# Local attention's projections and its rounds put into one block

## The reference, cut to what matters

```python
g = x @ Wg.T + bg
v = x @ Wv.T + bv
# per head:
dot = jnp.einsum('bhid,bhjd->bhij', g, g)
corr = dot / (nrm[..., :, None] * nrm[..., None, :] + 1e-08)
corr = (corr * m + 1.0) / 2.0                 # m: j <= i and j >= i - 128
gene_means = jnp.mean(corr, axis=3)
denom = gene_means + 0.5
sum_inv = jnp.sum(1.0 / denom, axis=2, keepdims=True)
gene_fitness = 1.0 / (denom * sum_inv)
weighted = corr * gene_fitness[..., None]
attn = softmax(weighted * m + (1.0 - m) * NEG)
out = attn @ v
```

## Time and profile before

| what | value |
|---|---|
| median of three runs | 2852.92 us (2851.32 to 2854.34) |
| the profiled execution | 2852.49 us |
| its span | 2850.7 us |
| PE busy | 2644.2 us (93%) |
| DVE busy | 1940.7 us (68%) |
| ACT, POOL busy | 802.1, 799.2 us (28%, 28%) |
| mean granted clock of PE | 0.97 |

### The profile page before, as it was taken

How to read it: one execution, slowest core, us unless ns; L and a number is a source line. 1 busy time by engine, 2 the same in 40 slices (tenths; PEclk the granted TensorE clock), 3 DMA queues, 4 the chain that set the end, 5 groups by cost and what they waited for, 6 DMA issues and landing times. The chain is left out here.

```text
span 2850.7 us, 39066 instructions
## 1 busy us (share of the span) xinstructions
PE 2644.2 (93%) x14094; PEld 1608.4 (56%) x14094; DVE 1940.7 (68%) x3503; ACT 802.1 (28%) x1239; POOL 799.2 (28%) x795
## 2 busy tenths in 40 slices
PE   7999988999998999679888859999999999999996
PEld 3444544555554455335445526777777777777774
DVE  4788404666666344268888737888888888888884
ACT  1111312333332233267777601111111111111110
POOL 1222104544553333356666411111111111111000
PEclk9999999999999999889999979999999999999998
DMA  5344130000000233323233430111111111111111
GB/s 161 132 161 154 60 109 1 1 1 1 1 1 0 79 101 102 91 91 91 84 88 90 144 76 25 44 45 43 43 43 43 44 44 45 44 45 44 41 37 33
DMA packets 220884, 177.07 MB, mean 62 GB/s; under 512 B 40171, under 2 KB 185579, under 8 KB 219670
## 3 DMA queue, kind: packets, MB, share of 16 engines
q1 hardware_dynamic: 183710, 147.87, 17.3%
q10 hardware_dynamic: 36984, 26.71, 3.5%
HBM read 90.51 MB, written 52.43 MB: 50 GB/s over the span
## 5 line engine op out<-in xcount | busy, mean ns | idle before, releaser
L1974 PE MATMUL bank<-tiles,tl_XQT 128*128 128x512 f32 (+1 forms) x768 | 331.7, 575 | 7.5 <-DMA tl_XQT<-tl_QB 4.8
L1989 PE MATMUL bank<-tiles,tl_HT 128*128 128x512 f32 x704 | 317.8, 607 | 20.2 <-DMA tl_HT<-tl_tmp 20.2
L1979 PE MATMUL bank<-tiles,tl_XQT 128*128 128x512 f32 (+1 forms) x768 | 317.9, 557 | 0.0
L1989 PEld LDWEIGHTS bank<-tiles,tl_HT 128*128 128x128 f32 x704 | 225.2, 324 | 97.2 <-issue 30.2
L1974 PEld LDWEIGHTS bank<-tiles,tl_XQT 128*128 128x128 f32 x768 | 232.5, 310 | 73.9 <-issue 16.3
L1979 PEld LDWEIGHTS bank<-tiles,tl_XQT 128*128 128x128 f32 x768 | 236.7, 308 | 65.6
L1477 POOL TENSOR_SCALAR_AFFINE_SELECT tiles<-tiles 128x512 f32<-128x512 f32 x256 | 173.0, 678 | 194.5 <-ACT tiles L1650 138.3
L1927 POOL TENSOR_TENSOR tl_rs<-tl_ve,mhalf 128x1 f32<-128x1 f32 x32 | 17.7, 552 | 593.0 <-DVE tl_ve L2082 593.0
L2023 ACT ACTIVATE tl_HQ<-bank 128x512 f32<-128x512 f32 (+1 forms) x96 | 54.0, 562 | 427.5 <-PE bank L1974 405.7
L1710 DVE SCALAR_TENSOR_TENSOR tiles<-tiles,bank 128x1024 f32<-128x1024 f32 (+1 forms) x128 | 141.6, 1147 | 4.9 <-PE bank L1559 2.7
L1919 POOL TENSOR_TENSOR tl_rs<-tl_ve,mhalf 128x1 f32<-128x1 f32 x32 | 19.9, 623 | 426.6 <-DVE tl_ve L2064 426.6
(11 more groups left out here) (287 smaller groups left out, 5069.8 us busy)
## 6 DMA issues: line engine op xcount, KB each, us to landing
tl_HT<-tl_tmp SPq DMA_DIRECT2D x256, 44.0 KB, 1.9
tl_HT<-tl_tmp ACTq DMA_DIRECT2D x256, 44.0 KB, 1.9
fp_weights<-space_quant ACTq DMA_DIRECT2D x33, 256.0 KB, 2.2
X<-in_x SPq DMA_DIRECT2D x8, 1024.0 KB, 11.9
v<-la_VS SPq DMA_DIRECT2D x32, 256.0 KB, 2.3
unit_g<-la_GH SPq DMA_DIRECT2D x32, 256.0 KB, 2.9
unit_gT<-la_GT SPq DMA_DIRECT2D x32, 256.0 KB, 3.2
la_GN<-unit_g SPq DMA_DIRECT2D x128, 64.0 KB, 2.2
```

Of the source, the lines that this page charges most:

```text
L1974: mm = e.matmul(bank[(2 * q) % 3][:, 0:w], chunk(XQT[n % 2], c), WgT[q][:, :, c, :], start=(c == 0), stop=(c == C - 1))
L1979: mm = e.matmul(bank[(2 * q + 1) % 3][:, 0:w], chunk(XQT[n % 2], c), WuT[q][:, :, c, :], start=(c == 0), stop=(c == C - 1))
L1989: mm = e.matmul(bank[DOWN][:, :], chunk(HT, q), WdT[:, q, :], start=(q == 0), stop=(q == IC - 1))
```

## The change

- `local_attention_projections` goes away as a stage. Its work is in `local_attention`, half a tile per round: `projected(p)` gives the tile m = p // 4 + 10 and the part. Part 0 has the transposition of x of tile m + 1 and the matmuls with Wg of tile m; part 1 the transposition of the unit vectors of tile m - 1 and the matmuls with Wv of tile m. The log norms are kept for a batch element (8 tiles) and split, transposed and stored once per batch element.
- The rounds now start at s = -56: 22 rounds (p = -44 to -2) have projections alone, then each round has half a tile, until p = 90.
- The projections' PSUM banks are 0 to 3, one each for x, g, v and the unit vectors, which are those of the dot products. PE's `projections` waits until DVE has taken this round's dot products; `dots` waits until ACT and DVE have emptied the projections' banks. `projections` stands between `arguments(p + 1)` and `attend(x + 1)`.
- AHEAD is 12 (was 16), RING 16 (was 20); the gather runs two steps behind the arguments (was four), and z, sums, inverse and scaled come earlier in a chunk: sums at p = 6 and 10 of a chunk (were 8 and 12), the first scaling at 10 (was 14), the second at 12 (was 16).
- ACT does `exp(s + 1)` ahead of `tanh(p + 1)`, and the normaliser last. POOL has the same order of masks and the power behind them.
- The constants are made during the first rounds, before p = 0.
- The output weights and the down weights are loaded at p = 98, the latter into the eleven buffers of the projections; gate and up weights at s = 118, 122 and 124.
- The local weights get a home (`k.home`) that outlives `Spaces`, and Wo and the folded weights go there afterwards.

The core of the diff:

```diff
+RING = 16
+BUFFERS = 11
+GATE_AT = [4 * q * SLOT for q in range(3)]
+UP_AT = [4 * q * SLOT + C * w for q, (_, w) in enumerate(PIECES)]
+DOWN_AT = RING * SLOT
...
+LAST_IN = (3, 7, 10)
...
+    AHEAD, LAG, BEFORE = 12, 2, 10
...
+        XT = [piece(n).rearrange("p (c t) -> p c t", c=C) for n in range(2)]
+        Gs, SG, GH, VS, GQ = ([piece(n + i) for i in range(m)] for n, m in ((2, 2), (4, 1), (5, 2), (7, 2), (9, 2)))
...
+        ROUNDS = range(-AHEAD - 4 * BEFORE - 4, NS + LAG + 2, 2)
+        projected = lambda p: (p // 4 + BEFORE, p // 2 % 2)
+        batch_next = lambda p: (p + 2) // (G * C) if (p + 2) % (G * C) == 0 and 0 <= p + 2 < NS else None
+        batch_of = lambda m: m // G - 1 if m % G == 0 and 0 < m <= NT else None
...
+                def projections_stored(m, part):
+                    if part == 0:
+                        if tile(m - 1):
+                            n = m - 1
+                            e.wait_ge(s_vc.sem, s_vc.at(n + 1))
+                            e.dma_start(by_tile(k.VNd, n), VS[n % 2].rearrange("p (c d) -> p c d", c=C)).then_inc(d_v[n % 2].sem, 16)
+                        if tile(m - 2):
+                            n = m - 2
+                            e.wait_ge(s_gc.sem, s_gc.at(n + 1))
+                            e.dma_start(k.GTd[:, n // G * C:(n // G + 1) * C, n % G * P:(n % G + 1) * P],
+                                        GQ[n % 2].rearrange("p (c t) -> p c t", c=C)).then_inc(d_gq[n % 2].sem, 16)
+                        b = batch_of(m - 1)
+                        if b is not None:
+                            for h in range(2):
+                                e.wait_ge(s_yc.sem, s_yc.at(2 * b + h + 1))
+                                e.dma_start(k.YD[b][:, half_of(h)], YT[h][:, :]).then_inc(d_y[h].sem, 16)
+                    elif tile(m - 1):
+                        n = m - 1
+                        e.wait_ge(s_gh.sem, s_gh.at(n + 1))
+                        e.dma_start(by_tile(k.GNd, n), GH[n % 2].rearrange("p (c d) -> p c d", c=C)).then_inc(d_gh[n % 2].sem, 16)
...
+                def weights_after_projections():
+                    for s in (s_v, s_gh, s_s2, s_gt):
+                        e.wait_ge(s.sem, s.at(NT))
+                    VB, WoT = k.out_weights
+                    e.dma_start(VB, k.SW[:, VO_AT:FOLDED]).then_inc(s_next.sem, 16)
+                    e.dma_start(WoT[:, :, :], chunked(a["L1_attn_Wo_T"])).then_inc(s_next.sem, 16)
+                    for j in range(4):
+                        e.dma_start(k.tiles[32 * j:32 * j + 32, DOWN_AT:DOWN_AT + IC * D].rearrange("p (i d) -> p i d", d=D),
+                                    down_rows[32 * IC * j:32 * IC * (j + 1), :].rearrange("(i p) d -> p i d", p=32)).then_inc(k.d_wd, 16)
...
+                    b = batch_next(p)
+                    if b is not None:
+                        batch_stored(b)
+                        if b:
+                            e.wait_ge(s_arg.sem, s_arg.at(G * (C * b - 1)))
+                        load_rows(C * b)
+                    projections_stored(*projected(p))
...
+                        m, part = projected(x + AHEAD)
+                        e.wait_ge(s_xc.sem, s_xc.at(min(m + 1 + part, NT)))
+                        e.wait_ge(s_ga.sem, s_ga.at(min(m + part, NT)))
+                        e.wait_ge(s_vc.sem, s_vc.at(min(m, NT)))
+                        e.wait_ge(s_gc.sem, s_gc.at(min(m - 1, NT)))
+                        e.wait_ge(s_yc.sem, s_yc.at(2 * min((m - 1) // G, B)))
...
+                def projections(m, part, s):
+                    e.wait_ge(s_u.sem, s_u.at(min(s + 2, NS)))
+                    if part == 0:
+                        if tile(m + 1):
+                            n = m + 1
+                            e.wait_ge(s_xc.sem, s_xc.at(n))
+                            e.wait_ge(s_yc.sem, s_yc.at(2 * ((m - 1) // G)))
+                            for c in range(C):
+                                mm = e.transpose(bank[0][:, c * P:(c + 1) * P], tile_x(n)[:, c * P:(c + 1) * P], k.ident[:, :])
+                            mm.then_inc(s_t.sem, 1)
+                        if tile(m):
+                            e.wait_ge(s_xc.sem, s_xc.at(m + 1))
+                            e.wait_ge(s_ga.sem, s_ga.at(m))
+                            for c in range(C):
+                                mm = e.matmul(bank[1][:, :], XT[m % 2][:, c, :], WgT[:, c, :], start=(c == 0), stop=(c == C - 1))
+                            mm.then_inc(s_g.sem, 1)
+                    else:
+                        if tile(m - 1):
+                            n = m - 1
+                            e.wait_ge(s_gh.sem, s_gh.at(n + 1))
+                            e.wait_ge(s_gc.sem, s_gc.at(n))
+                            for c in range(C):
+                                mm = e.transpose(bank[3][:, c * P:(c + 1) * P], GH[n % 2][:, c * P:(c + 1) * P], k.ident[:, :])
+                            mm.then_inc(s_gt.sem, 1)
+                        if tile(m):
+                            e.wait_ge(s_vc.sem, s_vc.at(m))
+                            for c in range(C):
+                                mm = e.matmul(bank[2][:, :], XT[m % 2][:, c, :], WvT[:, c, :], start=(c == 0), stop=(c == C - 1))
+                            mm.then_inc(s_v.sem, 1)
+                        b = batch_of(m)
+                        if b is not None:
+                            e.wait_ge(s_y.sem, s_y.at(b + 1))
+                            e.wait_ge(s_xc.sem, s_xc.at(min(m + 2, NT)))
+                            e.wait_ge(s_ga.sem, s_ga.at(min(m + 1, NT)))
+                            for h in range(2):
+                                for q in range(HG):
+                                    g = HG * h + q
+                                    mm = e.transpose(bank[h][0:3 * H, q * P:(q + 1) * P],
+                                                     Y3[:, g * H:(g + 1) * H, :].rearrange("p h s -> p (h s)"), k.ident[:, :])
+                                mm.then_inc(s_yt.sem, 1)
...
-                    chains = [(at_chunk(p, G + HG * h), h) for h in range(2)]
+                    chains = [(at_chunk(p, 6 + HG * h), h) for h in range(2)]
...
-                    if there(p - 4):
-                        gather(p - 4)
-                        gather(p - 3)
+                    if there(p - 2):
+                        gather(p - 2)
+                        gather(p - 1)
...
+                    projections(*projected(p), s)
...
                         exp(s)
+                        exp(s + 1)
                     if there(p):
                         tanh(p + 1)
+                    if part == 0:
+                        if tile(m + 1):
+                            x_transposed(m + 1)
+                        if b is not None:
+                            logarithms(b)
+                    else:
+                        if tile(m - 1):
+                            unit_transposed(m - 1)
+                        if tile(m):
+                            v_scaled(m)
+                        if b is not None:
+                            y_transposed(b)
                     if there(x) and not first(x):
                         normaliser(x // 2)
-                    if there(s):
-                        exp(s + 1)
...
+                    if p == 0:
+                        constants()
                     if there(x):
                         out(x // 2)
                     if there(s):
                         scores(s)
                         scores(s + 1)
-                    if here(G + 6) is not None:
-                        scaled(here(G + 6), 0)
-                    if here(2 * G) is not None:
-                        scaled(here(2 * G), 1)
-                    if here(HG + 2) is not None:
-                        z(here(HG + 2), 0)
-                    if here(G + 2) is not None:
-                        z(here(G + 2), 1)
-                        inverse(here(G + 2), 0)
-                    if here(G + 4) is not None:
-                        inverse(here(G + 4), 1)
-                        share(here(G + 4))
+                    if part == 1 and tile(m):
+                        norms(m)
+                    if here(12) is not None:
+                        scaled(here(12), 1)
                     if here(HG) is not None:
-                        tile_sums(here(HG), 0)
+                        z(here(HG), 0)
+                        tile_sums(here(HG), 1)
+                    if here(6) is not None:
+                        inverse(here(6), 0)
                     if here(G) is not None:
-                        tile_sums(here(G), 1)
+                        z(here(G), 1)
+                    if here(0) is not None:
+                        tile_sums(here(0), 0)
+                    if here(10) is not None:
+                        inverse(here(10), 1)
+                        share(here(10))
+                        scaled(here(10), 0)
+                    if part == 0:
```

(7 more changed lines are left out.)

370 lines of the change are left out of this document (144 added, 226 removed).

## The result

| | before | after |
|---|---|---|
| median of the plain runs | 2852.12 us (2850.71 to 2854.34) | 2824.14 us (2822.50 to 2826.00) |
| ratio, 95% interval | | 0.9901 (0.9884 to 0.9919) |
| span of the profiled execution | 2850.7 us | 2822.0 us |
| start of the block to the first dot products | 315.5 us | 129.0 us |
| the 38 rounds s = 0 to 74 | 236.6 us | 386.9 us |

A forecast was written before the change was run, and what follows sets the result against it. PE was taken to bound the projections, while steady attention left it holes (busy 88.42 of 100 us). From 2852.5 us, -192.4 + 151.2 - 2 + 4 - 10.9 = -50.1 gave 2802 us, range 2774 to 2834.

The forecast's parts named there:

- the half-price lock: POOL's power blocks DVE at half its full price, slack absorbing the rest: 2830 us; chance 0.18 shared with non-sharing rounds.
- rounds that don't share at all: Double rounds keep all old holes plus new waits, 10.9 us each: 2829 us; chance 0.18 shared with the half-price lock.
- (a, b): Prologue and run-up together: 123.1 us to the first dot products against 315.5 before, 192.4 us less.
- (c): 38 rounds s = 0 to 74 with attention and half tiles: 10.2 us each against 6.22, 151.2 us more.
- (d): Rounds s = 76 to 130 without projections: 2 us gained; bulk weight load at p = 98: 4 us lost (0 to 8).
- (e): End of the block: last store no longer queues behind the down weights, 10.9 us saved.
- (a): Prologue, p = -44 to -2: ten projection tiles, 82.1 us, plus 2 us for the first batch's rows; constants covered.
- (b): Run-up of the attention ring: six rounds instead of eight, 6.5 us each with about 0.5 of waits, 39 us.
- The sharing itself gives next to nothing: Rounds with both cost what the stages cost apart (6.22 + 3.9 = 10.1), new hand-overs eating the closed holes.
- PE at full (9.6): PE stays full in double rounds because copies hide behind `attend`; the tail keeps 5 us more: 2774 us; chance 0.14.
- The lock: POOL's 2.9 us power blocks DVE; full price 55 us over 19 tiles, 2857 us, chance 0.02.
- Rival 3: Banks 0 to 3: PE waits for both late DVE scores and the copy; 12.2 us per round, 2878 us; chance 0.06.

The follow-up runs named there:

- first experiment: The changed kernel with the six output and down weight transfers issued one per round from p = 98 to 108, not all at p = 98: 2805.57 us.
- the last experiment: The early Tanh kernel (2801.4 us) with a batch's log-norm transpositions on TensorE and copies on ScalarE moved ahead of V: 2801.73 us.
- third experiment: The changed kernel with BEFORE = 34 instead of 10, so all 32 projection tiles run ahead of the first attention round: 2830.53 us.
- early Tanh: The kernel with first and last weights spread one transfer per round (2802.5 us), plus an unread one-column Tanh right behind the logarithm: 2801.36 us.
- the experiment: The changed kernel with POOL doing a second, unread power of the same shape after each inverse norm: 2822.48 us.

## Why the prediction was right and wrong

The forecast was 2802 and the measurement is 2824.14: inside the stated range, outside the 2783 to 2821 that I gave the forecast itself. The range went up to 2834 for the half-price lock and for rounds that don't share at all (both about 2830, with a chance of 0.18), and neither came true: the rounds with both took the 10.2 us that I had. So the right range is luck. Where the 22 us went is in the table, against what the traces show, in us of span (the start of the block, 1.1 later, and the stages behind, 1.9 longer, make up the 28.7, to rounding):

| term | said | measured |
|---|---|---|
| (a, b) to the first dot products | -192.4 | -186.5 |
| (c) 38 rounds with both | +151.2 | +150.3 |
| (d) tail without the bulk load | -2 | -4.4 (first experiment) |
| (d) bulk load | +4 (0 to 8) | +16.5 |
| (e) end | -10.9 | -7.7 |

**(a) held.** The first arguments run at 1011.65, 83.5 us after the block's start; I had 84.1 with the 2 us for the rows' round trip. The round trip costs nothing, though barely: the last experiment turned it into 1.02 us. The parts are a little other than mine. A plain tile takes 7.75 us, and the tile with the log norms of a batch 1.9 more, which my 4 us for the start covered. The constants cost nothing either; without the cover of further tiles 10.6 us come back (third experiment).

**(b) failed by 6.5 us.** PE's busy part was near what I had, 37.36 us against 36. The waits were 8.1 us against my 3. I had taken "about 0.5 of waits" from nothing but the thought that a half tile fills them. But the half tile stands behind `arguments(p + 1)`, which waits for the tanh of p: 6.6 of the 8.1 us by PE's waits, 2.5 of them at p = 0, with a table load in it. Three of the 6.5 us are that table load (the versions without it and with the early Tanh); the rest did not go away with another order on PE.

**(c) held**, by its steps as well: busy 9.59 per round for my 9.48 + 0.1, waits 0.6 for my 0.2 + 0.4. The copy's cover by `attend(x + 1)` is 0.5 us (I had 0.58), and without it a round is 10.71. "The sharing itself gives next to nothing" is right for these rounds: it costs 3.3 us in 387. A batch costs 2.4 us, not 1.5. The table loads are 1.4 of the 2.4 (the version without them), so with two of them in my 1.5 I had priced them too low.

**The rivals.** PE at full (9.6) was rightly set against: the dot products wait 0.5 us per round. The lock, with a chance of 0.02 in full and a share of 0.18 in half, did not show. The trace of the change bears out the reason that I had given: beside the 19 powers in these rounds DVE has no operation with two SBUF inputs. Whether larger ones would be held up is not shown; the ten small ones of the experiment were not. Rival 3 was right in place, price (12.2; 12.16 measured) and effect (slower than before), but needs another order than the one written. That the price agrees so well is luck, since its cause is only in part what I gave: PE's waits for DVE's late scores are 25.1 us of it, while those before the dot products, for ACT's copy behind a late tanh among others, grew by some 41. Its total, 2914.65, is above my 2878 because of 37.5 us in the tail, where the call waits for the scores with nothing to do.

**(d) failed on the size of the bulk load**, and this is the main error: 12.5 of the 21 us of span that were missing. The step was "some 14 us stand before the next GN loads", against a lead of 8 to 10 us. From the first issue (1484.05) to the landing of the load that PE wanted (1507.08) it is 23.0 us, 9 more than my 14. And PE wanted it 7.7 us after that first issue, 2 earlier than my 10. Of these 7.7 us the load itself had only 3.3, for SP needs 4.4 us to issue the weights in front of it.

The 14 us were nowhere in the rows that I had. They mean some 340 GB/s for all of it, but the down pieces go to 32 partitions each, and the row "0.91 of DMA time at 172 GB/s" was of just these. SP's wait of 13.0 us was of these four pieces alone in front of one store, and 1.8 MB more now stand ahead of them. The throughput of the kernel after is 365 to 394 GB/s while Wo lands, then about 190 to 230 for the down pieces: 2.8 MB at 200 GB/s are 14 us, with 1.8 MB at some 370 GB/s it is 19, and the loads behind landed when that was over. The Trainium skill, "SBUF — State Buffer", section "Can I just issue two DMAs to hit both halves?", says that only a transfer over all 128 partitions reaches all ports; these rates agree with it, though no run varies the partitions alone.

Without the bulk load the tail gave 4.4 us, twice what I had, although the round s = 78 takes 4.7 us more than its like, which I had overlooked: I had put the batches' cost into the rounds with both alone.

**(e) failed by 3 us.** The last store lands quickly, as I had said. But I had taken the last output to stay where it was. Its store is issued 12.9 us after the dot products of s = 126, where it was 8.8 us in the kernel before, because the V loads of the last tiles stood behind pairs of weight pieces. With the pieces a round apart it is 9.8 us, and the end comes 3.4 us earlier than with the first weights alone spread.

What stays open: the rest of the run-up's waits (3 us), how far a power holds up larger operations of DVE with two SBUF inputs, and whether another order on DVE would take the 4 us out of the round s = 78.

## What to carry to other kernels

The price of a bulk load is not its bytes over the best rate but everything that is issued behind it on its queue, at the rate that rows of this very transfer show. Six pieces together cost 16 us that one piece per round doesn't. When an operation is moved between engines' hand-written orders, follow every hand-over through the other engine's order as well, and look for the waits that it takes along where it has nothing to do: half a tile moved by one call on PE cost 112 us, 75 in the rounds with a half tile (a tanh in front of a copy on ACT, and DVE's scores) and 37 in those of the tail, which have none. And sharing rounds pays where an engine is idle for latency (run-up, round trips), not where it is nearly full already.
